# A two-layer pipeline over 16 sequences: the hardware loop over the inner twelve is written out, with constant wait counts

## The chip, the cores and the metric

The kernel runs on one core of one Trainium2 chip. The metric is the device time of one execution in microseconds (us), where less is better. The core has five engines that run their own instruction streams and meet only through semaphores: TensorE (PE) does matmuls and transposes, VectorE (DVE) and ScalarE (ACT) do element-wise work and reductions, GpSimd (POOL) some element-wise work, SyncE (SP) issues the DMA transfers.

## The reference

The input x has 16 sequences of 512 tokens with 128 channels. Two layers are applied, each as `x = x + attention(norm(x)) + ffn(norm(x))`:

```python
x = L0_attn_x                                   # (16, 512, 128) f32
xn = _layernorm(x)
x = x + _L0_attn_ref(xn, ...) + _L0_ffn_ref(xn, ...)
xn = _layernorm(x)
x = x + _L1_attn_ref(xn, ...) + _L1_ffn_ref(xn, ...)
```

- `_L0_attn_ref`: 16 heads of 64, scores `k q^T` with a causal mask, softmax, values, and an output projection of 1024 to 128.
- `_L0_ffn_ref`: again a block of its own: layernorm, a causal convolution of width 3, 16 heads of 8 with rotary tables, softmax, projection, residual; then layernorm, a router that takes one of 4 experts, each expert `silu(gate) * value @ proj` with a width of 512.
- `_L1_attn_ref`: 16 heads of 8 in blocks of 64 keys, with a running maximum and sum whose formula is kept as written.
- `_L1_ffn_ref`: gate, up and down products of inputs that are rounded to 4-bit floats in blocks of 16.

All sequences are independent and get the same work; the shapes never change from one to the next.

## The kernel before

One body of the kernel, the function `run(i, nxt, nn, prv)`, works on four sequences at once, each in another stage. Sequence `i` goes through the large attention and the experts ("dense"), sequence `nxt` (one later) through the small rotary attention ("ahead"), `nn` (two later) is loaded, normalised, convolved and projected ("early"), and `prv` (one earlier) is in the second layer ("behind"). The order of all steps of all four is written out by hand in the list `ORDER` (lines 127 to 177). Every engine walks through this one list (`walk`, line 206) and issues those steps that it has a part in. So each engine has a fixed in-order program, and all that moves an engine along is its waits on semaphores.

The semaphores are never reset. Each counts up over the whole kernel, by a fixed number per sequence (the tables `DENSE`, `EARLY`, `AHEAD`, `BEHIND`). A wait therefore needs the number "sequence times count per sequence plus so many". `counter` (line 191) makes it: a sequence is a pair `(reg, more)`. Where `reg` is a Python integer the number is a constant inside the instruction. Where `reg` is the loop's register, the engine executes a register addition first (line 200, the lines 605 to 629 on POOL) and the wait compares with that register.

`pipeline` (line 485 on) lays the bodies out, on every engine alike: three bodies that fill the pipeline, a full body for i = 1 with constants, a hardware loop for i = 2 to 13 (`eng.Fori`, line 492), one body without a new sequence (i = 14) and two that drain. Since each engine jumps back by itself, there is no barrier at the loop's end.

Names that the prediction uses, in the order in which they stand around the seam between two bodies. At the end of a body: the router's matmul of `nxt` (`route`, PE line 1524), the copy of the second layer's result out (`store_out`, SP line 577), the arg-max of the router (DVE lines 1128 to 1140). At the head of the next: PE projects the first two pairs of heads of `i` (`project_kq`, line 1337, `value_side`, line 1349); ACT copies the router's input (`begin`, line 692), then takes these projections out of PSUM (lines 703, 709); DVE takes over the accumulated result (`take_over`, line 1147); then PE computes the first masked scores (`scores`, line 1359). In the middle of a body SP issues the three small copies of `shift_rows` (line 555) and, later, 18 copies of split keys and queries (`split`, line 566). The store of line 577 occurs once in each body from i = 1 on, and is used as a mark for the end of a body; the first of them, at 611.47 us, ends the body of i = 1. The copies of line 555 are the mark for the middle.

Of the kernel before, what the change touches and what calls it, by code (L numbers as in the profile page):

```python
# [214 lines left out]
def build_layers(nc, w, x, consts, out):  # L215
    B = x.shape[0]
    with ExitStack() as ctx:
# [267 lines left out]
        def pipeline(eng, run):  # L485

            run(None, None, (0, 0), None)
            run(None, (0, 0), (0, 1), None)
            run((0, 0), (0, 1), (0, 2), None)  # L490
            run((0, 1), (0, 2), (0, 3), (0, 0))
            with eng.Fori(2, B - 2) as i:
                run((i, 0), (i, 1), (i, 2), (i, -1))
            run((0, B - 2), (0, B - 1), None, (0, B - 3))
            run((0, B - 1), None, None, (0, B - 2))
            run(None, None, None, (0, B - 1))

        @block.sync
        def _(sp):
# [39 lines left out]
            def run(i, nxt, nn, prv):  # L539
# [49 lines left out]
                if prv is not None:  # L589
                    store_out()  # L590

            pipeline(sp, run)
            sp.wait_ge(out_stored, B * BEHIND["out_stored"])

        @block.gpsimd
        def _(pool):
# [62 lines left out]

            prep_over(pool)  # L660
            pipeline(pool, run)

        @block.scalar
        def _(act):
# [21 lines left out]
            def run(i, nxt, nn, prv):  # L686
# [142 lines left out]
                walk(steps, i, nxt, nn, prv)  # L829

            pipeline(act, run)

        @block.vector
# [823 lines left out]
```

## Time and profile before

| | us |
|---|---|
| median of 3 runs | 3894.04 (3883.72 to 3913.90) |
| the profiled execution, its own time | 3885.07 |
| its span, first to last instruction | 3883.0 |
| PE busy with matmuls | 3406.5 (88% of the span) |
| DVE busy | 2506.9 (65%) |
| ACT busy | 1754.1 (45%) |
| POOL busy | 381.3 (10%) |

A busy share is a mean over the whole span. Register, branch and semaphore instructions are not counted as busy: time that an engine spends on them shows as idle time "until issue", which means that nothing that the profile shows was waited for.
### The profile page before, as it was taken

The numbers are of one execution on the slowest core, as the hardware profiler recorded it, in microseconds if no ns is written. First come the engines' busy times: TensorE is split into PE (matmuls) and PEld (weight loads), VectorE is DVE, ScalarE is ACT, GpSimd is POOL, SyncE is SP. The second block draws the span as 40 slices with busy tenths as digits, with TensorE's granted clock in tenths as the row PEclk, the third lists the DMA queues.
The fourth block names the chain that finished last, engine by engine and source line by source line (L and its number), as shares of the span: only waits on it lengthen the run. The fifth ranks groups of instructions, "written<-read, shape, count | busy, mean of one in ns | idle before, by whom it ended". The sixth has DMA issues, their size and how long they took to land.

```text
span 3883.0 us, 62655 instructions
## 1 busy us (share of the span) xinstructions
PE 3406.5 (88%) x20319; PEld 1876.6 (48%) x20319; DVE 2506.9 (65%) x5526; ACT 1754.1 (45%) x4156; POOL 381.3 (10%) x676
## 2 busy tenths in 40 slices
PE   2689998989999898999989899898989989898864
PEld 1245455544545455454545545454555545454432
DVE  4555677657767666776766677677667767756453
ACT  0254554535454454545545454544545455454421
POOL 0000200102020010202001020200102020110201
PEclk6799999989999999999989999999999999999975
DMA  4111102020200202020020202002020200200000
GB/s 100 18 25 13 22 2 36 2 37 2 27 11 2 36 2 37 2 29 9 5 33 2 37 2 29 8 7 32 2 37 2 30 7 5 30 1 4 1 3 3
DMA packets 78817, 66.93 MB, mean 17 GB/s; under 512 B 8626, under 2 KB 75124, under 8 KB 78452
## 3 DMA queue, kind: packets, MB, share of 16 engines
q1 hardware_dynamic: 78452, 62.41, 11.2%
q8 instruction: 187, 3.06, 0.4%
q14 instruction: 178, 1.46, 0.1%
HBM read 15.47 MB, written 4.19 MB: 5 GB/s over the span
## 4 chain that ended last, share of the span: by engine, by line
PE 68%; DVE 12%; issue 8%; POOL 6%; ACT 5%; SPq 1%; DMA 1%; POOLq 0%; DVEq 0%; ACTq 0%
PE ps L1376 7%; PE ps L1394 5%; PE ps L1359 5%; PE ps L1387 5%; PE ps L1415 5%; PE ps L1494 4%; PE ps L1479 4%; PE ps L1558 3%; PE ps L1337 3%; PE ps L1580 3%; PE ps L1403 3%; DVE nma L1020 2%; PE ps L1460 2%; PE ps L1349 2%; POOL vn L614 2%
## 5 line engine op out<-in xcount | busy, mean ns | idle before, releaser
L718 ACT ACTIVATE share_a<-ps,nma 128x128 f32<-128x128 f32 (+3 forms) x1024 | 531.3, 524 | 432.3 <-DVE nma L1020 430.2
L1020 DVE TENSOR_REDUCE nma<-ps 128x2 f32<-128x256 f32 (+3 forms) x512 | 420.8, 825 | 416.0 <-PE ps L1362 408.2
L1084 DVE TENSOR_REDUCE nmx<-ps 128x1 f32<-128x384 f32 (+3 forms) x704 | 426.7, 634 | 201.9 <-PE ps L1462 198.2
L760 ACT ACTIVATE share_z<-ps 128x512 f32<-128x512 f32 (+1 forms) x704 | 367.7, 558 | 407.6 <-PE ps L1481 405.4
L614 POOL TENSOR_TENSOR vn<-va,rla 128x512 f32<-128x512 f32 x128 | 133.7, 1044 | 3060.7 <-DVE rla L976 3060.7
L1376 PE MATMUL ps<-share_a,vn 128*64 128x512 f32 (+3 forms) x2048 | 324.1, 461 | 37.1 <-POOL vn L614 35.0
L1337 PE MATMUL ps<-xnTd,wkqT 128*128 128x512 f32 x512 | 279.2, 672 | 70.1 <-issue 47.3
L729 ACT ACTIVATE share_g<-ps 128x512 f32<-128x512 f32 x256 | 153.0, 598 | 361.1 <-PE ps L1387 359.9
L1460 PE MATMUL ps<-kst,qst 96*128 96x128 bf16 (+3 forms) x1024 | 264.5, 311 | 56.1 <-DMA kst<-part 36.4
L1387 PE MATMUL ps<-h2Td,wgv 128*128 128x512 f32 x512 | 267.8, 605 | 2.8 <-ACT share_a L718 2.8
L1394 PE MATMUL ps<-h2Td,wgv 128*128 128x512 f32 x512 | 269.1, 607 | 0.0
L980 DVE SCALAR_TENSOR_TENSOR share_g<-share_g,ps 128x512 f32<-128x512 f32 x256 | 175.5, 686 | 138.5 <-ACT share_g L729 132.8
L1479 PE MATMUL ps<-qst,kst 99*128 99x512 bf16 (+3 forms) x1024 | 253.1, 303 | 12.2 <-ACT share_z L760 8.0
L1415 PE MATMUL ps<-wdn,share_a 128*128 128x128 f32 x2048 | 243.1, 277 | 21.3 <-DVE share_a L993 21.3
L1376 PEld LDWEIGHTS ps<-share_a,vn 128*64 128x64 f32 x2048 | 144.4, 143 | 234.5 <-issue 195.7
L1415 PEld LDWEIGHTS ps<-wdn,share_a 128*128 128x128 f32 x2048 | 236.6, 193 | 43.0 <-issue 33.8
L1359 PE MATMUL ps<-kq_odd 64*128 64x128 f32 (+3 forms) x1024 | 216.7, 501 | 41.6 <-ACT share_a L718 35.5
L993 DVE SCALAR_TENSOR_TENSOR share_a<-share_g,ps 128x512 f32<-128x512 f32 x256 | 175.7, 686 | 105.1 <-PE ps L1394 96.9
L1359 PE MATMUL ps<-share_g 64*128 64x128 f32 (+3 forms) x1024 | 209.7, 486 | 29.9 <-ACT share_a L718 21.3
L718 ACT ACTIVATION_READ_ACCUMULATOR share_a<-ps,nma 128x1 f32 x1024 | 202.5, 198 | 0.0
L1462 PE MATMUL ps<-up_b,ident_b 128*128 128x128 bf16 x1024 | 201.5, 225 | 0.0
L1479 PEld LDWEIGHTS ps<-qst,kst 99*128 99x128 bf16 x1024 | 99.3, 98 | 205.2 <-ACT share_z L760 98.6
(220 smaller groups left out, 5607.3 us busy)
## 6 DMA issues: line engine op xcount, KB each, us to landing
qst<-part SPq DMA_DIRECT2D x144, 128.0 KB
kst<-part SPq DMA_DIRECT2D x144, 128.0 KB
xin<-in_L_attn_x SPq DMA_DIRECT2D x16, 256.0 KB, 12.0
xk<-xn SPq DMA_DIRECT2D x16, 256.0 KB, 18.8
xres<-in_L_attn_x SPq DMA_DIRECT2D x16, 256.0 KB, 2.8
out<-xn SPq DMA_DIRECT2D x16, 256.0 KB, 11.9
wgv<-in_L_ffn_expert_wv SPq DMA_DIRECT2D x1, 2048.0 KB
qst<-share_h SPq DMA_DIRECT2D x48, 16.0 KB, 2.2
```

The source lines that it names most:

```text
L718: activation(pa[:, h % 4, OFF[t]:OFF[t] + P * (t + 1)], ps[:, b + k, 0:P * (t + 1)], ACT.Exp, bias=nma[:, h, t:t + 1], accum_out=la[:, h, ...
L760: activation(pt[:, n % 2, h % 4:h % 4 + k, 0:wd], src, ACT.Exp, scale=SCALE_B)\
L1020: v.tensor_reduce(nma[:, 2 * p:2 * p + 2, t], ps[:, b:b + 2, 0:P * (t + 1)], AX.X, ALU.max, negate=True).then_inc(amax, 1)
L1084: v.tensor_reduce(nmx[:, h:h + k, t], src, AX.X, ALU.max, negate=True).then_inc(bmax_ready, 1)
L1337: ins = mm(ps[:, b + z, :], wkqT[:, z, 2 * DA * p:2 * DA * (p + 1)], xnTd[:, :], start=True, stop=True)
L1359: mm(ps[:, b + k, 0:P * (t + 1)], kq[p % 2][rows, 0, tile(t)], kq[p % 2][rows, 1, 0:P * (t + 1)], start=True, stop=False)
L1376: ins = mm(ps[DA * k:DA * k + DA, 4, 0:P * (t + 1)], vn[:, h % 4, t, :], pa[:, h % 4, OFF[t]:OFF[t] + P * (t + 1)], start=(t == NT - 1), s ...
L1387: mm(ps[:, (2 * n) % 3, :], wgv[:, e, c * P:(c + 1) * P], h2Td[:, :], start=True, stop=True).then_inc(gate_psum, 1)
L1394: mm(ps[:, (2 * n + 1) % 3, :], wgv[:, e, DFF + c * P:DFF + (c + 1) * P], h2Td[:, :], start=True, stop=True).then_inc(value_psum, 1)
L1415: ins = mm(ps[:, 3, tile(t)], ym[:, e % 2, c, tile(t)], wdn[:, e, c, :], start=(c == 0), stop=(c == CHUNKS - 1))
L1460: mm(ps[:, b, o:o + wd], qst[0:SHIFT_ROW, h, tile(t)], kst[0:SHIFT_ROW, h, 0:wd], start=True, stop=False)
L1479: mm(ps[:, b, o:o + wd], kst[0:SHIFT_ROW + PARTS, h, tile(j)], qst[0:SHIFT_ROW + PARTS, h, j * P:T], start=True, stop=False)
```

## The change

The hardware loop becomes a Python loop, so that the body is emitted twelve times, for i = 2 to 13, on each of the five engines. The pair that stands for a sequence now has an integer in its second place and a zero in its first, so `counter` returns constants everywhere, and the addresses of the loads and stores in HBM are constants too.

```diff
@@ -489,8 +489,8 @@
             run(None, (0, 0), (0, 1), None)
             run((0, 0), (0, 1), (0, 2), None)
             run((0, 1), (0, 2), (0, 3), (0, 0))
-            with eng.Fori(2, B - 2) as i:
-                run((i, 0), (i, 1), (i, 2), (i, -1))
+            for i in range(2, B - 2):
+                run((0, i), (0, i + 1), (0, i + 2), (0, i - 1))
             run((0, B - 2), (0, B - 1), None, (0, B - 3))
             run((0, B - 1), None, None, (0, B - 2))
             run(None, None, None, (0, B - 1))
```

Where the loop begins on ACT, the instructions change as follows (one piece of the difference, "-" before, "+" after; a row is a line of the kernel, the operation and its operands).

```order
 L822 COPY share_s<-ps 128x384
 L777 ACTIVATE share_h<-ps,ln 128x512
-L492 UNCONDITIONAL_BRANCH
-L492 ISA
-L200 REGISTER_ALU
 L692 COPY h2Td<-share_h 128x512
-L200 ISA
-L703 COPY share_g<-ps 128x1024
-L200 REGISTER_ALU
-L709 COPY va<-ps 128x512
-L200 REGISTER_ALU
-L200 ISA
```

The branch into the loop, the loop's head and the register additions go; the copies stay, in the same order. PE's rows at the loop's end stand like this before (the row after the branch is the body of i = 14; in all iterations but the last the branch goes back to the loop's head):

```order
L1616 MATMUL ps<-wdT,share_s 128x128 x12
L200 REGISTER_ALU
L1314 MATMUL ps<-ident,xh 128x128 x4
L200 REGISTER_ALU
L1524 MATMUL ps<-wrt,share_h 128x4 x4
L492 REGISTER_ALU
L492 COMPARE_AND_BRANCH
L1337 MATMUL ps<-xnTd,wkqT 128x512 x2
L1349 MATMUL ps<-wvT,xnTd 128x128 x4
```

And PE's rows at the seam between two of the twelve bodies after:

```order
L1616 MATMUL ps<-wdT,share_s 128x128 x12
L1314 MATMUL ps<-ident,xh 128x128 x4
L1524 MATMUL ps<-wrt,share_h 128x4 x4
L1337 MATMUL ps<-xnTd,wkqT 128x512 x2
L1349 MATMUL ps<-wvT,xnTd 128x128 x4
L1337 MATMUL ps<-xnTd,wkqT 128x512 x2
L1359 MATMUL ps<-share_g 128x128 x2
```

No engine has a compare-and-branch left. PE's program grows from 2642 to 7693 such rows, DVE's from 1734 to 4603, ACT's from 864 to 2234; PE had 230 rows of register additions, DVE 264 and ACT 149, and all are gone. No matmul, copy, reduction or transfer is added, dropped or moved.

## Rows read from the trace of the kernel before

**Rows 1.** The profile's page: span, busy time by engine, chain that ended last.
```profile
span 3883.0 us, 62655 instructions
PE 3406.5 (88%) x20319; PEld 1876.6 (48%) x20319; DVE 2506.9 (65%) x5526; ACT 1754.1 (45%) x4156; POOL 381.3 (10%) x676
...
PE 68%; DVE 12%; issue 8%; POOL 6%; ACT 5%; SPq 1%; DMA 1%; POOLq 0%; DVEq 0%; ACTq 0%
```

**Rows 2.** Stretches between stores: from:to, length, busy times, granted clock, DMA share, GB/s.
```profile
611.47:3325.56 2714.09, 2497.36 (x15207) 1388.69 (x15207) 1854.30 (x4116) 1307.58 (x3109) 285.90 (x504) 0.97 0.12 17
830.28:3325.56 2495.28, 2291.30 (x13939) 1273.84 (x13938) 1699.77 (x3773) 1198.55 (x2850) 262.08 (x462) 0.97 0.12 17
611.47:830.28 218.81, 206.06 (x1270) 114.85 (x1270) 154.53 (x343) 109.03 (x259) 23.82 (x42) 0.98 0.13 17
830.28:1062.99 232.71, 207.77 (x1269) 116.11 (x1268) 154.52 (x343) 109.20 (x259) 23.82 (x42) 0.96 0.12 16
2195.86:2418.69 222.83, 205.60 (x1269) 114.95 (x1268) 154.45 (x343) 108.85 (x259) 23.83 (x42) 0.98 0.12 16
```

**Rows 3.** Second halves of bodies, from line 555's first copy to the store.
```profile
510.93:611.47 100.54, 96.85 (x636) 58.30 (x634) 78.29 (x195) 42.18 (x83) 1.02 (x1) 1.00 0.18 21
729.24:830.28 101.04, 97.15 (x638) 58.56 (x636) 78.18 (x195) 42.02 (x82) 0.92 (x1) 1.00 0.18 21
3224.52:3325.56 101.04, 97.15 (x638) 58.55 (x636) 78.17 (x195) 42.29 (x83) 0.92 (x1) 1.00 0.18 21
```

**Rows 4.** First halves, from the store to line 555's first copy of the next body.
```profile
611.47:729.24 117.77, 108.91 (x633) 56.29 (x634) 76.34 (x148) 67.01 (x177) 22.90 (x42) 0.97 0.08 14
830.28:961.95 131.67, 110.63 (x632) 57.57 (x632) 76.34 (x148) 67.18 (x177) 22.90 (x42) 0.92 0.07 12
2195.86:2317.65 121.79, 108.45 (x632) 56.40 (x632) 76.29 (x148) 66.83 (x177) 22.91 (x42) 0.97 0.06 13
3325.56:3441.78 116.22, 107.23 (x632) 55.62 (x632) 76.23 (x148) 66.72 (x177) 22.77 (x42) 0.99 0.07 11
```

**Rows 5.** Waits between 393 and 3325 us: who waited, total, times, longest.
```profile
ACT h2Td L692 <- issue: 111.0, 11, 11.0
...
DVE xp L1147 <- issue: 100.7, 11, 10.3
...
PE ps L1337 <- issue: 47.3, 11, 11.8
```

**Rows 6.** The chain of waits across the fourth jump back: start, length, what.
```profile
1520.25 0.06 DVEq L492
1520.32 9.42 issue
1529.74 0.05 DVEq L492
```

**Rows 7.** Timeline at three seams: start, length, engine, operation, idle before.
```profile
612.34 1.96 PE L1337 MATMUL ps<-xnTd,wkqT 128*128 128x512 f32 x4
...
842.79 3.77 PE L1337 MATMUL ps<-xnTd,wkqT 128*128 128x512 f32 x4 [11.76 <-issue]
...
3326.17 1.96 PE L1337 MATMUL ps<-xnTd,wkqT 128*128 128x512 f32 x4
```

**Rows 8.** The body of i = 1, by PE's line 1524 to line 1524.
```profile
393.89:611.42 217.53, 205.69 (x1267) 114.48 (x1267) 154.43 (x343) 109.13 (x260) 23.80 (x42) 0.98 0.14 18
```

**Rows 9.** Waits between 393 and 611.4 us: the longest single wait until issue.
```profile
PEld ps L1359 <- issue: 8.2, 17, 2.5
```

**Rows 10.** Instruction queues in 393.07 to 611.47: packets, MB, share of 16 engines.
```profile
q8 instruction: 10, 0.16, 0.3%
q14 instruction: 6, 0.05, 0.1%
```

**Rows 11.** Instruction queues in 1062.99 to 1291.46.
```profile
q8 instruction: 13, 0.21, 0.4%
q14 instruction: 13, 0.11, 0.2%
```

## The prediction

> **What bounds the kernel now.** I read the page first. PE is busy for 88% of the span, and the chain that ended last is 68% PE, with 8% "issue", time for which the profile knows no cause [rows 1]. So PE sets the pace, and the question is what stands between its matmuls. A change of the loop must show at the seams between bodies, so the next view was the table of stretches, cut at the store that ends each body. Twelve bodies (i = 2 to 13) take 2714.09 us. The first of them, which is entered in sequence, takes 218.81 us; the eleven that are entered by the jump back take 2495.28 us, 226.84 each, from 222.83 to 232.71, with the same number of matmuls to within the two or three that a trace can miss [rows 2]. The reader is to see that the loop's code costs nothing by itself the first time round: something happens at the jump.
>
> The third view halves each body. The second half, from the copies of `shift_rows` to the store, takes 101.04 us in the first looped body and 101.04 in the last, and 100.54 in the body of i = 1, which is written with constants [rows 3]. The first half takes 117.77 us in the body entered in sequence, 131.67 and 121.79 in two of the jumped ones, 116.22 in the body of i = 14, whose first half is the same work with constants [rows 4]. All the variation lies in the first half.
>
> The fourth view, the list of waits, names it. Eleven times, as often as the loop jumps back, ACT stands before its first instruction of a body for 10.1 us (111.0 / 11), DVE for 9.2 (100.7 / 11) and PE for 4.3 (47.3 / 11, once 11.8), each "until issue" [rows 5]. The chain shows the place: DVE's branch of line 492 takes 0.06 us, then there is nothing for 9.42 us, then the head of the loop, 0.05 us [rows 6]. Where a body is entered or left in sequence, PE's first matmul has no idle time before it at all; after the first jump it has 11.76 us, and then runs 3.77 us instead of 1.96, at the lower of the clock's two levels [rows 7].
>
> **The change, part by part.**
>
> *The jumps.* Eleven jumps back go. Their price is not the sum of the engines' idle times, since these lie beside each other; it is what the first halves grow by. The eleven jumped bodies have 2495.28 − 11 × 101.04 = 1383.84 us in first halves, 125.80 each, against 117.77 entered in sequence with the same instructions [rows 2 to 4]: 8.03 us a jump, 88.3 us in all. That is less than ACT's 10.1 because PE can do its first projections while ACT is away, and it contains what the lower clock costs after the gap (granted 0.92 in that half after the first jump, 0.97 in the entered one [rows 4]).
>
> *The register additions and the branches' own time.* They go from all twelve bodies. The second half shrinks from 101.04 to 100.54, the first from 117.77 to 116.22 [rows 3, 4]: 2.05 us a body, 24.6 us in all. A second measure is smaller: the body of i = 1, from router matmul to router matmul, takes 217.53 us [rows 8], where 116.22 + 100.54 is 216.76. By it a body shrinks by 218.81 − 217.53 = 1.28 us, 15.4 us in all. The two differ by a little clock or DMA luck that I can't part. I take the middle, a body of 217.15 us.
>
> *Rows that now hold several waits in one instruction, constant addresses for SP.* They are in the same measure, since the bodies of i = 1 and 14 have them.
>
> *POOL.* Its jump cannot cost anything: POOL is busy 10% of the span [rows 1] and its first work in a body comes long after the seam.
>
> *Fill and drain.* Everything up to 611.47 us and after 3325.56 keeps its instructions: nothing. That zero needs no cover, since only the place of these instructions in memory moves.
>
> *More code.* The programs grow about threefold on PE. What this costs can be bounded from the trace. In the body of i = 1, straight code, the instruction queues move 10 and 6 packets [rows 10]; in a looped body 13 and 13 [rows 11]. So the looped body is fetched anew every time already, and straight code asks for less, not more. In that straight body no computing engine has idle time until issue of over 2.5 us at once [rows 9], and neither ACT nor DVE any. From below the cost is nothing, or a small gain through fewer packets; from above, a fetch that is not ahead of its engine costs what a jump costs it, up to 11.0 us on ACT and 11.8 on PE [rows 5]. I take nothing, by the row that is nearest, the straight body itself.
>
> *Sum.* 2714.09 − 12 × 217.15 = 108.3 us saved, against the profiled execution's 3885.07: 3776.8. That execution was 9 us under the median of the three runs shown and near the fastest; PE's gap at the jump varied between its mean of 4.3 and 11.8 within this one execution, so part of the spread among runs should be the jumps' own and go with them. I say 3778.
>
> Here a rule speaks against so large a gain. The Trainium skill, "Advanced Engine Details and Errata", section Control Flow Timing, gives about 108 ns for a compare-and-branch; by that figure the eleven jumps are worth an estimated 1.2 us. The branch itself in this trace, 0.06 us, agrees; the 9.42 us behind it are not in that rule [rows 6]. The Trainium skill, "Runtime: NRT & Kernel Launch", section Instruction fetch mechanics, says that instructions are fetched ahead in sequence, in blocks of 16 KiB, and that a taken branch to a block that isn't held stalls until it is fetched. By that rule the trace agrees: the gaps stand only behind jumps, and the packets are 0.16 MB / 10 = 16 KB on one of the two queues [rows 10].
>
> **The rivals.**
>
> *Some fetches are late in straight code (7%), still faster.* The borders of blocks now fall at another place in each of the twelve bodies, sometimes under the 18 copies of `split`, and into the densest stretches of PE. If each body had one wait like PE's mean of 4.3 us on its path, 12 × 4.3 = 51.6 us come back: 3828. Against it stand three bodies and halves of straight code without such a gap.
>
> *The gap belongs to the place, not to the jump (3%).* At each seam a load and a store are on their way, and instruction packets could be late for that. Then only the register additions would go, 15.4 to 24.6 us, which gives 3860 to 3870. Against it: at 611.47 us the same load and store are issued, and there is no gap [rows 7].
>
> *Slower (3%).* The mechanism is the same late fetch, but on ACT or PE at a full price of 10.1 to 11.8 us and more than once a body. The gain in a body is 226.17 (2714.09 / 12) − 217.15 = 9.0 us, so it decides from 9.0 us of exposed wait a body; two waits of 10.1 make 12 × (20.2 − 9.0) = 134 us on top, 4019. Even if all 10 packets of the fuller queue are PE's, the code in one lasts it about 22 us (217 / 10), twice the longest gap seen; that speaks against it.
>
> *That the change doesn't do what it says* is excluded by the instruction rows: no branch and no register addition is left.
>
> **How the numbers follow.** The forecast, all gaps gone and no new ones, has 87%. Its own range: with every body as long as the entered one, 218.81, 2625.7 us for the twelve, or 3797; with every body at 116.22 + 100.54 = 216.76, 3772. Differences between executions, which spanned 30 us before, add 15 us on either side: 3757 to 3812. The range for 8 in 10 reaches up towards the first rival: 3756 to 3820. A measurement of this kernel can tell about 1%, 39 us, from no change. Faster by over 1% are the forecast and the first rival, 94%; the second lies within 1%, 3%; slower 3%.
>
> **What would show it.** In the profile after, ACT's line 692, DVE's line 1147 and PE's first matmul of line 1337 have no idle time until issue at any seam; stores follow each other every 216 to 219 us, all eleven intervals within 2 us; the stretch from store to store over the twelve bodies is about 2606 us; second halves take 100.5 us; the instruction queues move about 10 and 6 packets a body; PE's share of the span rises to about 90%. The granted clock loses the half-speed stretches just behind each seam and keeps one late in the first half. It would be wrong if idle time until issue of several us turned up elsewhere in a body, at a place that wanders from body to body, or if the first halves stayed above 120 us without a gap.

## The result, and the profile after

The written-out kernel takes 3782.43 us (median of 4 runs, 3777.36 to 3790.12), the kernel before, run beside it, 3902.40 (3883.72 to 3913.90). The ratio is 0.970, with a 95% interval of 0.967 to 0.973. The forecast was 3778 us, range 3756 to 3820. The profiled execution took 3783.69 us; before it was 3885.07, one of the shorter ones of that kernel. So the medians lie 120.0 us apart and the two profiled executions 101.4; what is read from profiles below explains the second figure.

The first lines of the page of the profile after, which answer to [rows 1], and its instruction queues:

```profile
span 3781.9 us, 53946 instructions
...
PE 3371.3 (89%) x20319; PEld 1861.5 (49%) x20319; DVE 2505.3 (66%) x5526; ACT 1754.6 (46%) x4156; POOL 380.2 (10%) x676
...
q8 instruction: 161, 2.64, 0.3%
q14 instruction: 101, 0.83, 0.1%
...
PE 72%; DVE 13%; POOL 6%; ACT 4%; issue 3%; SPq 1%; DMA 1%; POOLq 0%; DVEq 0%; ACTq 0%
```

The same 20319 matmuls, 5526 DVE and 4156 ACT instructions ran. 8709 other instructions are gone, "issue" in the chain that ended last fell from 8% to 3%, and although PE's, DVE's and ACT's programs are two and a half to three times as long, the queues fetched less.

The stretches between stores of the profile after (from:to, length, busy times, granted clock, DMA share, GB/s): all twelve bodies, then the longest of them but one and one of the shortest, which answer to [rows 2]; the second and first halves of a body, which answer to [rows 3, 4].

```profile
609.28:3222.74 2613.46, 2462.88 (x15205) 1374.55 (x15205) 1852.83 (x4116) 1308.38 (x3109) 284.99 (x504) 0.99 0.12 17
826.25:1045.58 219.33, 207.22 (x1268) 114.88 (x1268) 154.38 (x343) 109.01 (x260) 23.75 (x42) 0.98 0.12 17
1045.58:1261.27 215.69, 203.05 (x1268) 113.71 (x1268) 154.41 (x343) 109.07 (x260) 23.75 (x42) 1.00 0.12 20
...
725.73:826.25 100.52, 96.83 (x636) 58.29 (x634) 78.25 (x195) 42.18 (x83) 1.02 (x1) 1.00 0.18 21
...
826.25:945.05 118.80, 110.38 (x633) 56.58 (x634) 76.12 (x148) 66.89 (x177) 22.73 (x42) 0.96 0.08 13
1045.58:1160.73 115.15, 106.20 (x633) 55.43 (x634) 76.13 (x148) 66.89 (x177) 22.72 (x42) 1.00 0.08 14
```

The twelve bodies took 2714.09 us and take 2613.46: 100.6 us less, and the whole span (3883.0 and 3781.9) is 101.1 us less, so the gain lies there. Second halves take 100.52 to 100.55, as in the straight body before (100.54). First halves differ by up to 3.65 us, and only with the clock: 115.15 us where it was granted in full, 118.80 at 0.96.

The timeline of one seam of the profile after (start, length, engine, operation, idle time before), which answers to [rows 7]:

```profile
1045.54 1.06 PE L1524 MATMUL ps<-wrt,share_h 128*128 128x4 f32 x8 [0.87 <-ACT share_h L777]
1045.57 0.62 ACT L692 COPY h2Td<-share_h 128x512 f32<-128x512 f32 x1
...
1046.45 1.96 PE L1337 MATMUL ps<-xnTd,wkqT 128*128 128x512 f32 x4
...
1048.41 0.43 DVE L1147 COPY xp<-xacc 128x512 f32<-128x512 f32 x1
```

ACT, PE and DVE go on without idle time. None of the three waits of [rows 5] is left anywhere between 393 and 3325 us.

### The profile page after: what moved, and what is told of

The parts are those of the page before. It is cut to its first block, busy times and chain, and to the rows that moved or that the text cites. A ratio compares the mean times of both kernels' runs of the same rounds, so it can differ in the third digit from the quotient of the medians.

```text
span 3781.9 us, 53946 instructions
## 1 busy us (share of the span) xinstructions
PE 3371.3 (89%) x20319; PEld 1861.5 (49%) x20319; DVE 2505.3 (66%) x5526; ACT 1754.6 (46%) x4156; POOL 380.2 (10%) x676
## 4 chain that ended last, share of the span: by engine, by line
PE 72%; DVE 13%; POOL 6%; ACT 4%; issue 3%; SPq 1%; DMA 1%; POOLq 0%; DVEq 0%; ACTq 0%
PE ps L1376 8%; PE ps L1359 6%; PE ps L1387 6%; PE ps L1394 6%; PE ps L1415 5%; PE ps L1494 5%; PE ps L1479 4%; PE ps L1337 4%; PE ps L1558 4%; DVE nma L1020 3%; PE ps L1580 3%; PE ps L1403 3%; PE ps L1349 3%; PE ps L1460 2%; PE ps L1362 2%
## 5 line engine op out<-in xcount | busy, mean ns | idle before, releaser
L1337 PE MATMUL ps<-xnTd,wkqT 128*128 128x512 f32 x512 | 255.2, 622 | 28.2 <-ACT share_a L718 28.2
L1479 PEld LDWEIGHTS ps<-qst,kst 99*128 99x128 bf16 x1024 | 99.3, 98 | 205.3 <-ACT share_z L760 101.4
## 6 DMA issues: line engine op xcount, KB each, us to landing
out<-xn SPq DMA_DIRECT2D x16, 256.0 KB, 11.8
```

The lines of the kernel that those rows point to most:

```text
L1337: ins = mm(ps[:, b + z, :], wkqT[:, z, 2 * DA * p:2 * DA * (p + 1)], xnTd[:, :], start=True, stop=True)
L1479: mm(ps[:, b, o:o + wd], kst[0:SHIFT_ROW + PARTS, h, tile(j)], qst[0:SHIFT_ROW + PARTS, h, j * P:T], start=True, stop=False)
```

## The experiments

All start from the written-out kernel and change the twelve inner bodies. Times are medians; bodies come from the profiled execution of each.

**Two bodies in the loop.**

```diff
-            for i in range(2, B - 2):
-                run((0, i), (0, i + 1), (0, i + 2), (0, i - 1))
+            if eng is nc.sync:
+                for i in range(2, B - 2):
+                    run((0, i), (0, i + 1), (0, i + 2), (0, i - 1))
+            else:
+                with eng.Fori(2, B - 3, 2) as i:
+                    for k in range(2):
+                        run((i, k), (i, k + 1), (i, k + 2), (i, k - 1))
```

> The loop is kept, but holds two bodies: 6 iterations, 5 jumps back instead of 11; waits still compare with registers (SP alone is written out with constants). Theory (each taken jump back costs about 8 us, the registers 1.3 to 2.05 us a body): the written-out kernel's 3782 + 5 x 8.0 + 12 x 1.3 to 2.05 = 3838 to 3847, and gaps of 9 to 11 us on ACT and DVE at every second seam only. Rival (the gap belongs to the seam, where a load and a store are issued, and goes only with the registers): gaps at all seams, about 3885 to 3902. Rival (a jump costs by the length of the code that it jumps over): 5 gaps twice as long, about 3880.

Measured: 3829.13 us (3815.04 to 3835.27). Three neighbouring bodies; the middle one is entered by a jump, the others in sequence. Below, the waits until issue (total, times, longest):

```profile
824.33:1042.42 218.09, 205.66 (x1269) 114.60 (x1269) 154.53 (x343) 108.95 (x259) 23.76 (x42) 0.98 0.13 18
1042.42:1267.61 225.19, 207.78 (x1268) 115.33 (x1269) 154.46 (x343) 108.87 (x260) 23.76 (x42) 0.97 0.12 16
1267.61:1485.91 218.30, 205.87 (x1268) 114.67 (x1269) 154.51 (x343) 108.94 (x259) 23.76 (x42) 0.98 0.12 18
```

```profile
ACT h2Td L697 <- issue: 43.8, 5, 9.2
DVE xp L1152 <- issue: 40.8, 5, 8.5
PE ps L1342 <- issue: 15.7, 5, 3.5
```

SP is written out with constants; the four other engines loop. Five jumps, five gaps, five long bodies, at every second seam. Both rivals fall: the seam has no gap without a jump, and a jump over twice the code costs no more. The five jumped bodies took 222.29 to 225.36 us, 224.64 on average, and the six second bodies of the iterations 218.31: a jump costs 6.3 us in this execution, which was the shortest of the four. The total is 9 us under the expected range.

**Six bodies in the loop.** The same edit, SP again written out, with `eng.Fori(2, B - 7, 6)` and `range(6)`.

> As the kernel with two bodies in the loop, but with six: 2 iterations, 1 jump back, all twelve bodies with register additions. Theory: 3782 + 1 x 8.0 + 12 x 1.3 to 2.05 = 3806 to 3815, second halves of 101.04 us. Rival (register additions are hidden, and only their neighbourhood with jumps made them look dear): 3790, second halves of 100.5.

Measured: 3802.13 us (3798.01 to 3805.59), 4 us under the range. The one jumped body and its neighbours:

```profile
1706.14:1925.09 218.95, 206.19 (x1271) 114.96 (x1271) 154.54 (x343) 108.95 (x259) 23.82 (x42) 0.98 0.13 18
1925.09:2153.10 228.01, 209.70 (x1267) 115.98 (x1267) 154.44 (x343) 109.34 (x260) 23.82 (x42) 0.96 0.11 16
2153.10:2371.59 218.49, 205.90 (x1268) 114.62 (x1269) 154.45 (x343) 109.19 (x260) 23.82 (x42) 0.98 0.12 18
```

The jump costs 9.4 us. The eleven others average 218.6 us, against 217.8 of the written-out kernel's profiled execution and 216.8 of a second one (below): with the registers a body is 0.8 to 1.9 us longer, and part of that is the clock, as said below. The rival that calls the registers free falls by the second halves, where the clock was granted in full: mostly 100.86 us against 100.53. They are not the 101.04 expected, since SP is written out here, and the loop on SP and POOL is worth 0.17 us of a second half (below). By the medians of this kernel and of the one with two bodies, which ran beside it, four jumps are worth 27.0 us, 6.8 each.

```diff
-            for i in range(2, B - 2):
-                run((0, i), (0, i + 1), (0, i + 2), (0, i - 1))
+            with nc.Fori(2, B - 2, engines=[eng.engine], hint_back_edge=True) as i:
+                run((i, 0), (i, 1), (i, 2), (i, -1))
```

Measured: 3836.98 us (3820.25 to 3867.30), between the two forecasts. The waits until issue show why:

```profile
PE ps L1337 <- issue: 53.1, 10, 8.1
DVE xp L1147 <- issue: 8.1, 12, 0.8
```

ACT's gap is gone and DVE's is down to 0.7 us each, so those gaps were late fetches of the jump's target. PE kept its gap at ten of eleven jumps, 5.3 us each, in this profiled execution, which took 3867.30 us and was the longest of the four. That the shorter ones had fewer gaps on PE is likely, since 3820 us leaves room for about three such gaps above the 3796 us of the kernel without any on PE (below), but only this one has a trace. At the eleventh it had none, and that body is as short as one entered in sequence; the eleven jumped bodies together took 2475.06 us:

```profile
831.49:3306.55 2475.06, 2282.28 (x13939) 1269.12 (x13938) 1700.06 (x3773) 1200.46 (x2850) 261.94 (x462) 0.97 0.12 17
1285.65:1504.06 218.41, 205.99 (x1269) 114.74 (x1269) 154.59 (x343) 109.11 (x260) 23.81 (x42) 0.98 0.12 18
```

**Branches that don't jump back.**

```diff
-            for i in range(2, B - 2):
-                run((0, i), (0, i + 1), (0, i + 2), (0, i - 1))
+            for k in range(2, B - 2):
+                with eng.Fori(k, k + 1) as i:
+                    run((i, 0), (i, 1), (i, 2), (i, -1))
```

> Twelve loops of one iteration each: at every seam each engine executes the register addition, the compare-and-branch, not taken, and an unconditional branch to the next instruction; counts are constants. Theory (only a jump away from what is fetched in sequence costs): no gap over 0.5 us, 3782 + 12 x 0.2 = 3784. Rival (any branch makes the engine wait for its fetch): gaps of 9 to 11 us at all twelve seams, 3870 to 3880.

Measured: 3774.61 us (3768.16 to 3776.39), and no idle time until issue over 0.2 us on PE's matmuls, DVE, ACT or POOL. (PE's weight loads have waits of 2.5 us until issue in every run, the straight body before included [rows 9].) A branch that is not taken, or goes on to the next instruction, costs nothing that can be seen. The time was even 8 us under the written-out kernel's; this was tried again (below).

**One engine alone in the loop.** Four kernels with this edit, the condition being `eng is nc.scalar`, `nc.tensor`, `nc.vector`, and the last with `nc.sync or nc.gpsimd`:

```diff
+            if eng is nc.scalar:
+                with eng.Fori(2, B - 2) as i:
+                    run((i, 0), (i, 1), (i, 2), (i, -1))
+            else:
+                for i in range(2, B - 2): ...
```

> ACT alone keeps the hardware loop and its register additions; the four other engines are written out. Theory (what ends last at the seam is ACT: its 10.1 us gap makes the copies of the projections late, PE's first scores wait for them): the first scores come 10 to 12 us after the store instead of 5.3, a jump costs 5 to 7 us, 3782 + 11 x 6 = 3840 to 3865. Rival (PE's own gap is what counts): 3790.

> PE alone keeps the hardware loop and its register additions. Theory: its mean gap of 4.3 us is on the path in full, since PE is the bound, and some half-clock time behind it; registers on PE some 1 us a body: 3782 + 11 x 4.3 + 12 = 3830 to 3845. Rival (PE's gap lies beside ACT's and costs nothing by itself): 3790.

> DVE alone keeps the hardware loop and its register additions. Theory: DVE comes 9.2 us late to the maxima of the first scores, which stand some 4 us behind its take-over; the scores ring is only two deep, so PE waits from there: a jump costs 5 to 7 us, as with ACT alone, and the three do not add up: 3782 + 11 x 6 = 3835 to 3860. Rival (DVE has slack in the first half, 65% busy): 3785 to 3795.

> SP and POOL keep the hardware loop and their register additions; PE, ACT and DVE are written out. Theory: neither has anything due at the seam, 3782 +- 8, no gap on the others. Rival (SP's load of the next input and the residual come late behind SP's jump): 3790 to 3850.

Measured: ACT alone 3866.61 us (3856.13 to 3877.83), PE alone 3877.92 (3852.83 to 3899.83), DVE alone 3885.13 (3876.44 to 3894.09), SP and POOL 3788.06 (3783.39 to 3790.63). The gaps, of the three kernels in turn, were near those of the full loop [rows 5], PE's without the one of 11.8 us:

```profile
ACT h2Td L696 <- issue: 114.3, 11, 11.9
```
```profile
PE ps L1341 <- issue: 36.7, 11, 3.6
```
```profile
DVE xp L1151 <- issue: 101.3, 11, 10.2
```

And the eleven jumped bodies of each, ACT, PE, DVE, to be set against the same eleven of the written-out kernel (last row, from its second profiled execution):

```profile
828.40:3307.10 2478.70, 2274.30 (x13938) 1275.97 (x13938) 1698.24 (x3773) 1199.20 (x2850) 261.23 (x462) 0.97 0.12 16
```
```profile
824.01:3295.13 2471.12, 2300.57 (x13938) 1276.08 (x13938) 1697.83 (x3773) 1200.21 (x2850) 261.26 (x462) 0.96 0.12 16
```
```profile
828.78:3327.52 2498.74, 2299.76 (x13938) 1271.34 (x13939) 1698.80 (x3773) 1199.93 (x2850) 261.88 (x462) 0.96 0.12 16
```
```profile
823.96:3209.49 2385.53, 2249.59 (x13938) 1255.01 (x13938) 1698.10 (x3773) 1199.31 (x2849) 261.91 (x462) 0.99 0.12 17
```

Per body (divided by 11) that is 225.3, 224.6 and 227.2 us against 216.9: 8.5 for ACT's jump alone, 7.8 for PE's, 10.3 for DVE's, while all engines together cost 226.8 − 216.9 = 10.0 [rows 2]. These four prices do not compare with each other as they stand: PE's profiled execution was its shortest of nine and that of the kernel before 17 us under its median, while ACT's and DVE's were at theirs. The row set against them is also of a short execution; against the 217.86 us of the first profile of the written-out kernel each is 1.0 us less. The medians of this group are fairer: above the kernel with only SP and POOL in the loop, 3788.06 us, ACT alone lies 78.6 us, PE alone 89.9, DVE alone 97.1, and the kernel before, run beside them, 114.1 (3902.20). The costs do not add up (265.6 against 114.1): the engines' gaps lie beside each other. Any one of the three makes the larger part of the loop's price by itself, ACT 69%, PE 79%, DVE 85%, and none makes all of it.

All three expectations were too low, ACT's by 2 us, PE's and DVE's by 25 to 33. The rows show what was left out for PE: its gap is 3.3 us, and its busy time is 4.6 us a body longer than in the last row (2300.57 against 2249.59 us over eleven) for the same matmuls, at a lower clock; together 8.0, near the price of 7.8. DVE's jump makes PE's busy time longer by as much, ACT's by 2.2. Nor is the price a fixed share of the gap. At the third jump back ACT stood for 3.99 us only, where it stood 9.7 to 11.9 at the ten others, and that body is as long as one without a jump:

```profile
1283.14 0.62 ACT L696 COPY h2Td<-share_h 128x512 f32<-128x512 f32 x1 [3.99 <-issue]
```
```profile
1279.24:1497.43 218.19, 205.90 (x1268) 114.42 (x1268) 154.31 (x343) 108.77 (x259) 23.75 (x42) 0.98 0.10 15
```

So 4 us of lateness on ACT cost nothing that can be seen at this seam, and the ten others, 226.05 us on average, cost 8 to 9 us each. SP's and POOL's jumps cost nothing that the medians can tell (3788.06 is within the expected 3782 ± 8).

**The same pause on PE, without a jump.**

```diff
             for i in range(2, B - 2):
+                if i > 2 and eng is nc.gpsimd:
+                    eng.wait_ge(zav_done, 8 * i)
+                    eng.wait_ge(h2T_ready, i + 1)
+                    for k in range(4):
+                        eng.tensor_tensor(vn[:, 0:2, :, :].rearrange("p k t d -> p (k t d)"),
+                                          cosT, sinT, ALU.mult).then_inc(spare_done, 1)
+                        eng.wait_ge(spare_done, 4 * (i - 3) + k + 1)
+                if i > 2 and eng is nc.tensor:
+                    eng.wait_ge(spare_done, 4 * (i - 2))
                 run((0, i), (0, i + 1), (0, i + 2), (0, i - 1))
```

> The written-out kernel, where at eleven seams PE's first matmul also waits for four multiplications on POOL (each about 1.04 us, begun when the router's input is ready), so that PE alone stands for about 3.5 us, with no jump and no late fetch anywhere. With PE alone in a loop, gaps of 3.3 us on PE made a body 8 us longer, and behind each there was more time at the lower clock. Theory (a pause on PE at this place costs its own length and some 4 to 5 us through the clock, whatever made the pause): bodies of 222 to 226 us, 3782 + 11 x 8 = 3855 to 3880. Rival (the extra 4 to 5 us come from PE's instructions being fetched late all along behind a jump): only the gap itself, bodies of 219 to 222 us, 3782 + 11 x 3.5 = 3820.

Measured: 3836.11 us (3831.12 to 3840.90), under the theory's range and over the rival's value. But PE stood for 4.41 us at each seam and not for the planned 3.5; with that pause the rival's sum is 3782 + 11 × 4.41 = 3830.5, and the measured time is nearer to it than to the theory. PE's first projections ran at the lower clock, as they do behind a jump:

```profile
1284.47 3.60 PE L1347 MATMUL ps<-xnTd,wkqT 128*128 128x512 f32 x4 [4.41 <-POOL vn L498]
```

Nine of the eleven bodies took 221.7 to 222.1 us like the first below, two took 225.3 and 225.5 like the second:

```profile
1279.05:1500.99 221.94, 204.83 (x1268) 114.44 (x1268) 157.42 (x343) 109.03 (x260) 28.89 (x46) 0.98 0.10 14
1053.76:1279.05 225.29, 209.04 (x1268) 115.70 (x1268) 157.43 (x343) 109.06 (x260) 28.89 (x46) 0.96 0.12 19
```

The two are the same work with the same pause; they part in the granted clock, 0.98 and 0.96. They first differ 19 us after the store, behind a wait of 1.8 us that both have:

```profile
1298.20 1.98 PE L1347 MATMUL ps<-xnTd,wkqT 128*128 128x512 f32 x4 [1.80 <-ACT share_a L728]
```
```profile
1072.92 3.56 PE L1347 MATMUL ps<-xnTd,wkqT 128*128 128x512 f32 x4 [1.81 <-ACT share_a L728]
```

The rest lies in the 32 us that begin 51 us after the store, for each of the two:

```profile
1330.05:1362.05 32.00, 25.63 (x154) 12.41 (x152) 27.72 (x45) 19.17 (x49) 11.83 (x33) 1.00 0.00 1
1104.76:1136.76 32.00, 26.60 (x147) 12.67 (x145) 25.68 (x42) 18.47 (x46) 8.47 (x32) 0.89 0.00 1
```

Against the same eleven bodies of the written-out kernel's second execution a body is 5.7 us longer: the pause of 4.4, and PE's busy time longer by 1.0 (2260.91 against 2249.59 us over eleven). The multiplications on POOL also made DVE's work of a first half 3 us longer (79.2 against 76.1 to 76.2), which that sum has no room for. So a pause without any jump brings the half-clock projections at the seam, and sometimes the later half-clock stretches that all eleven bodies of PE alone in a loop had in some measure. The theory's mechanism is shown, its size is not: a jump of PE cost 4.6 us of busy time beyond the gap, this pause 1.0. Why the later stretches came in all eleven bodies there and in two here is not settled, and something else of the jump may have a part in them.

**PE written out, the others in the hinted loop.** The hinted loop's edit, but with `eng is nc.tensor` written out.

> PE alone is written out; ACT, DVE, POOL and SP keep the loop, with the target of the jump back named at the loop's head. In the hinted loop ACT and DVE had no gap left and PE kept one of 5 us. Theory (the one gap that is left there makes the whole difference): no gap on any engine, 3782 to 3800, that is the written-out time plus up to 18 us for DVE's and ACT's register additions. Rival (hinted jumps cost elsewhere): 3820 to 3840.

Measured: 3795.70 us (3794.71 to 3797.07), in the theory's range. With PE's gap go 41 of the 55 to 59 us that the hinted loop had lost against the written-out kernel. This keeps the programs of ACT, DVE, POOL and SP at their old length for 13 to 18 us. "No gap" was not quite met: DVE had 0.7 us at each seam, and once 4.1 us until issue (1.8 in the hinted loop), in straight code. Both begin 9.2 us after the store that ends the loop's last body. No kernel without the hint has this second one; why it comes was not tried.

**The written-out kernel and the one-trip loops again, side by side.** Both unchanged.

> The written-out kernel unchanged, on the same chip as the others of this group, to be compared with the kernel of one-trip loops: 3782 +- 8.

> Twelve loops of one trip each, again, beside the written-out kernel. The first time it came out at 3774.6, 8 us under the other's 3782.4, from another group of runs. If the branches that aren't taken really shift the bodies against the clock's changes to advantage, it is again 5 to 10 us faster than the written-out kernel of this group, with half of the bodies free of half-clock time; if it was the scatter of runs, the two are within 3 us.

Measured: 3777.68 us (3767.47 to 3783.71) and 3773.66 (3767.35 to 3779.41); against the kernel before, ratios of 0.9691 (0.9658 to 0.9725) and 0.9684 (0.9652 to 0.9717). They lie 4.0 us apart, between the two values expected, with nearly the same ranges, so they can't be told apart, and no version is shown to beat the written-out one. In this profiled execution of it, its twelve bodies took 12 us less than in the first:

```profile
608.24:3209.49 2601.25, 2452.64 (x15205) 1368.72 (x15205) 1852.46 (x4116) 1308.39 (x3108) 285.72 (x504) 0.99 0.12 17
```

Six of them took 215.7 us and six 217.7 to 218.0, in turn; the one-trip loops beside it alternated in the same way. The same code has, in the same place, now no half-clock stretch and now one.

## Why the prediction was right

*The bodies.* 2714.09 − 12 × 217.15 = 108.3 us were forecast, 100.6 measured, with bodies of 217.79 us on average. In the second profiled execution they took 216.77, which would have made it 112.8. The term was right to within what the clock does from one execution to the next. The profiled execution is 6.9 us over the sum's 3776.8, and the bodies are 7.7 of that. Fill and drain, costed at nothing, moved by 2.2 us down and 1.7 us up (609.28 us against 611.47 before the first store, 559.2 against 557.4 behind the last): right.

*The base of the sum.* The sum starts from a profiled execution of 3885.07 us, 17 us under the median of the kernel before that ran beside the result. It was kept low on the argument that part of the spread among runs is the jumps' own and goes with them. That came out: four executions spread over 30.2 us before and 12.8 after, and in the last group 40.7 (11 executions) and 16.2 (6). With PE alone in the loop nine executions spread over 47.0 us, with DVE alone ten over 17.7. Taken from the median of 3902.40 the same 108.3 us would have given 3794, still in the range. That the forecast missed by only 4 us is in part luck.

*The jumps, 8.03 us each.* Right in size for that execution: 6.3 and 9.4 us in the loops of two and six bodies. The cause, the fetch of a target that isn't at hand, was argued before and is now shown: the price goes with the number of taken jumps, not with the seams and not in proportion to the length of the code, it is absent from branches that aren't taken, and ACT's and DVE's gaps vanish or nearly so when the target is named ahead. For PE, whose gap mostly stayed, it is shown only by the count of jumps. What the prediction had wrong in it was the picture of which gap counts. It explained 8.03 against ACT's 10.1 by PE's projections going on meanwhile. But PE has a gap of its own, and by the medians PE's jump alone makes 79% of the loop's price, DVE's alone 85% and ACT's alone 69%. About half of PE's and DVE's price is not idle time of PE at all but its matmuls taking longer at the lower clock.

*The registers, 1.28 to 2.05 us a body, 1.67 in the sum.* Mis-sized: about 1 us. The first halves must be compared at the same granted clock. At 0.97 the entered body before took 218.81 us [rows 2, 4], and the six such bodies of the second written-out execution 217.70 to 218.03, 0.8 to 1.1 less. The prediction's larger measure set a half at 0.97 against one at 0.99, and PE's busy time alone, 108.91 against 107.23 us, differs by more than the 1.55 us that it read as registers [rows 4]. In second halves, where the clock plays no part, the price is 0.52 us (101.04 against 100.52), and with ACT alone in the loop it was 0.23, SP and POOL 0.17, DVE 0.11, PE 0.00, which add up. The sum was some 8 us too generous here; that is within what the clock moved from one execution to the next (12 us).

*POOL's jump, costed at nothing.* Right: with SP and POOL in the loop 3788.06 us, no gap on the others, and 0.17 us in a second half.

*More code, costed at nothing.* Right: in the written-out kernel's two profiles PE's matmuls, DVE, ACT and POOL have no idle time until issue over 0.2 us, PE's weight loads none over the 2.5 us that they had before, and 120 and 74 packets were fetched in the twelve bodies, 10 and 6 a body as forecast, where the loop took 146 and 152. The slower rival has no sign in any run.

*The gap belongs to the place.* Excluded by the loop of two bodies and the one-trip loops.

*The branch's own time.* The prediction calls its row of 0.06 us in agreement with a figure of about 108 ns; it is near half of that. No term of the sum rests on it.

*What was to be seen.* The seams are without idle time, the second halves 100.5 us, PE's share 89% where about 90% was named. One sign was wrong: stores were to follow each other within 2 us, and the intervals went from 215.67 to 219.34. What moves them is the clock late in the first half, of which the two straight first halves before had given too small a sample.

## What to carry to other kernels

A hardware loop with a body as long as this one's (216 us; a looped body here was fetched anew each time) can pay for each taken jump back, here 6 to 10 us for each of 1 to 11 jumps; a loop with a short body was not tried. The jump of PE, ACT or DVE alone was enough to pay 69 to 85% of it, those of SP and POOL cost nothing that could be told. Look for it as idle time "until issue" at the first instruction of the body, as many times as the loop jumps; where one body of the same kind is already written out in the kernel, its length is the forecast, if the granted clock is the same in what is compared. Where the code must stay short, several bodies in one loop, or a written-out PE beside hinted loops on the others, get most of it back.

## What the runs showed of the hardware that was not expected

- Naming the branch's target ahead removed the gaps of ACT (10.1 us) and almost those of DVE (9.2 to 0.7) but only one of eleven on PE, where the others were 5.3 us on average, longer than without it (4.3). Why PE differs was not tried. DVE's extra gap behind the hinted loops' end, 1.8 and 4.1 us, is as open.
- The first jump of the kernel before cost PE 11.8 us and the ten others 3.6 on average; with PE alone in the loop, none cost more than 3.6. This stays open too.
- A short pause on PE costs more than its length: 7.8 us for one of 3.3 behind a jump, 5.7 for one of 4.4 without (against the other written-out profile 6.8 and 4.7). The projections behind it take 3.6 to 3.8 us instead of 1.96, at the lower of the clock's two levels. On ACT a pause of 4.0 us cost nothing, pauses of 9.7 to 11.9 us cost 8 to 9.
- Bodies with identical code and no gap take 215.7 us, or 217.0 to 219.3, by how much of their first half ran at the lower clock. The shortest and those of 217.7, which came in turn in two executions, part in a thinner stretch of PE's work, about 50 us into the body. In the profile after, with the same distance from the store, the two stretches of one body that kept the clock, then the two of one that lost it:

```profile
1093.58:1097.58 4.00, 2.07 (x15) 0.97 (x14) 3.61 (x10) 3.69 (x9) 0.00 (x0) 1.00 0.00 0
1097.58:1101.58 4.00, 1.82 (x10) 0.76 (x12) 4.00 (x7) 3.88 (x11) 1.04 (x1) 1.00 0.00 0
1309.27:1313.27 4.00, 2.07 (x15) 0.97 (x14) 3.61 (x10) 3.70 (x9) 0.00 (x0) 1.00 0.00 0
1313.27:1317.27 4.00, 2.29 (x8) 0.73 (x10) 4.00 (x7) 3.89 (x11) 1.04 (x1) 0.60 0.00 0
```
